# Causal mask of the first attention pass moved into constant rows of its contraction, with a reordered word list

## The reference

```python
att = jnp.einsum('bhqd,bhkd->bhqk', q, k) * (1.0 / math.sqrt(HS))
causal = jnp.tril(jnp.ones((Tx, Tx), bool))
att = jnp.where(causal[None, None, :, :], att, jnp.float32(-10000000000.0))
att = jax.nn.softmax(att, axis=-1)
y = jnp.einsum('bhqk,bhkd->bhqd', att, v)
y = y.transpose(0, 2, 1, 3).reshape(Bx, Tx, Cx)
return y @ Wp + bp
...
x = x + _layernorm(_L0_attn_ref(_layernorm(x, axis=-1), ...), axis=-1)
x = x + _layernorm(_L0_ffn_ref(_layernorm(x, axis=-1), ...), axis=-1)
```

## Time and profile before

| | |
|---|---|
| Median of 3 runs | 1155.79 us (1154.74 to 1156.82) |
| Span of the profiled execution | 1155.0 us |
| Own time of the profiled execution | not given apart from its span |
| TensorE busy | 1089.6 us, 94% |
| GpSimd busy | 833.4 us, 72% |
| VectorE busy | 832.6 us, 72% |
| ScalarE busy | 736.3 us, 64% |
| Mean granted TensorE clock | 0.967 |

### The profile page before, as it was taken

The page is one execution under the profiler, slowest core; times in us unless marked ns, Lnnn a source line. Parts: engine busy times, 40 slices in busy tenths (PEclk is TensorE's granted clock), DMA queues, the critical chain, the costliest instruction groups (busy, mean ns, idle before and its releaser), DMA issues.

```text
span 1155.0 us, 26958 instructions
## 1 busy us (share of the span) xinstructions
PE 1089.6 (94%) x8484; PEld 693.7 (60%) x8484; DVE 832.6 (72%) x2263; ACT 736.3 (64%) x1617; POOL 833.4 (72%) x972
## 2 busy tenths in 40 slices
...
GB/s 96 119 156 46 136 90 63 114 73 136 109 70 114 58 122 93 119 110 60 117 59 137 97 86 105 60 132 35 120 157 84 100 174 134 133 173 136 109 243 197
DMA packets 108885, 129.13 MB, mean 112 GB/s; under 512 B 17627, under 2 KB 89548, under 8 KB 104140
## 3 DMA queue, kind: packets, MB, share of 16 engines
...
q10 hardware_dynamic: 390, 0.10, 0.0%
...
## 4 chain that ended last, share of the span: by engine, by line
PE 89%; DVE 3%; DMA 2%; POOL 2%; SPq 2%; issue 1%; ACT 1%; POOLq 0%; DVEq 0%; ACTq 0%
PE heads_ps L1508 14%; PE score L1498 13%; PE wide L1536 12%; PE wide L1648 8%; PE wide L1474 6%; PE wide L1538 5%; PE score L1486 4%; PE wide L1631 3%; PE wide L1632 3%; PE score L1622 3%; PE misc L1516 3%; PE wide L1569 2%; DVE mx L1299 1%; PE wide L1576 1%; PE wide L1589 1%
## 5 line engine op out<-in xcount | busy, mean ns | idle before, releaser
L961 ACT ACTIVATE values<-score 128x512 f32<-128x512 f32 (+1 forms) x704 | 371.3, 558 | 122.7 <-PE score L1498 112.4
L1299 DVE TENSOR_REDUCE mx<-wide 128x2 f32<-128x1024 f32 (+3 forms) x384 | 392.9, 1042 | 73.4 <-PE wide L1538 69.0
L1536 PE MATMUL wide<-qk 72*128 72x512 bf16 (+3 forms) x1024 | 246.5, 305 | 8.0 <-DVE mx L1299 4.5
L871 POOL TENSOR_SCALAR_AFFINE_SELECT values<-values 128x512 f32<-128x512 f32 x256 | 173.9, 688 | 109.8 <-ACT values L961 108.4
L1498 PE MATMUL score<-qk 75*128 75x512 bf16 (+3 forms) x1024 | 230.1, 301 | 1.5 <-ACT values L961 0.8
L1538 PE MATMUL wide<-maskneg,identb 128*128 128x128 bf16 x1024 | 198.4, 222 | 0.0
L916 POOL DMA_INDIRECT token_scratch<-spread,e_id x144 | 137.7, 956 | 72.8 <-issue 52.9
L1508 PE MATMUL heads_ps<-values 128*32 128x512 f32 (+3 forms) x2048 | 175.4, 444 | 0.0
L860 POOL DMA_INDIRECT sorted_scratch<-zr,places x128 | 133.5, 1043 | 37.3 <-issue 28.5
L1536 PEld LDWEIGHTS wide<-qk 72*128 72x128 bf16 x1024 | 100.9, 99 | 79.4 <-issue 17.4
L1498 PEld LDWEIGHTS score<-qk 75*128 75x128 bf16 x1024 | 87.3, 98 | 97.6 <-ACT values L961 46.8
...
## 6 DMA issues: line engine op xcount, KB each, us to landing
...
```

The costliest lines, as they stand in the source:

```text
L871: nc.gpsimd.affine_select(out=prob[n][:, :, 0:P], in_=prob[n][:, :, 0:P], compare_op=ALU.is_ge, fill=0.0, base=0, pattern=[[0, HG], [1, P] ...
L961: nc.scalar.activation(free_ap(prob[kb][:, hs_[0], :], [[1, N * len(hs_)]]), score[SCORE_RING.buffer(b, step)][:, 0:N * len(hs_)], ACT.Exp ...
L1299: nc.vector.tensor_reduce(mx[:, h0:h0 + len(hs_), j:j + 1], src, axis=AX.X, op=ALU.max).then_inc(p1_max, 1)
L1536: nc.tensor.matmul(o, q4[e][0:ROWS, h, j * P:(j + 1) * P], k4[e][0:ROWS, h, 0:L], start=True, stop=False)
```

## The change

Outside the lists, the mask leaves the second matmul and becomes part of the contraction. 43 further rows (75 to 117, up to `MROWS` = 118) of `q4` and `k4` hold constant staircases, each row stepping at three positions, whose products are huge and negative above the diagonal. A pair of the first pass is now, for j over 0, a matmul with 72 rows over the j*128 columns that need no mask, and for every j one with 118 rows over the 128 columns of the diagonal block. `identb` and `maskneg` go. Since the 118 rows take in rows 72 to 74, those must be zero in `q4` until the maxima are laid in, so `shuffle` gets a seventh transfer for each half, which writes zeros. The staircases are made on GpSimd by six selects, four of them behind a wait, and copied once over all heads into partitions 64 to 127 of the four tiles: two copies of 8192 columns on VectorE (`stairs0`, `stairs2`) and two on ScalarE (`stairs1`, `stairs3`), as words of `START`. The two transfers of ones move from ScalarE to SyncE, in front of the first shuffles and behind waits for the copies. `ORDER` holds the same 160 words in a new order.

```diff
--- before.py
+++ after.py
@@ -20,13 +20,16 @@
 NPART = 3
 ROWS = NPART * NPART * HS
 SROWS = ROWS + NPART
+STAIR = 3
+MROWS = SROWS + -(-P // STAIR)
+HALF_ROWS = 64
+AHEAD, APART = 2.0 ** 34, 2.0 ** 46
 TOPK = 2
 ROW = P + 5
 EVEN = 112
 CAP = 72 * P
 BG = 4
 ROUND = 4
-NEG = -1e30
 EPS = 1e-5
 FILL = 12
 FIRST_FILL = 12
@@ -90,18 +93,17 @@
 
 
 ORDER = (
-    "s0.0 v3.1@-1 mask2.1 s0.1 p18@0 s0.2 p19@0 s0.3 v3.2@-1 v3.3@-1 p20@0 s0.4 s0.5 rnormal heads3@-1 p21@0 "
-    "mask2.2 s0.6 s0.7 p22@0 s0.8 K p23@0 s0.9 place s0.10 cos Y v0.0 M1@0 s1.0 s1.1 N1@0 p0 W mask2.3 s1.2 rstd "
-    "s1.3 v0.1 H2 v0.2 v0.3 zstats O1@0 s1.4 p1 normal mask3.0 U1 G1 s1.5 p2 s1.6 v1.0 p3 d3 s1.7 mask3.1 s1.8 p4 "
-    "mask3.2 d4 s1.9 p5 mask3.3 d5 s1.10 heads0 third0 s2.0 third1 p6 s2.1 p7 s2.2 v1.1 s2.3 p8 s2.4 v1.2 v1.3 "
-    "sin0@4 p9 d6 d7 s2.5 s2.6 U2 H0@-1 sin1@4 mask0.0@1 rstats mask0.1@1 G2 p10 sin2@4 heads1 s2.7 mask0.2@1 "
-    "mask0.3@1 stats d0@-1 s2.8 V s2.9 s2.10 p11 d1@-1 T v2.0 s3.0 mask1.0@1 p12 s3.1 d2@-1 M0 zrstd@0 v2.1 s3.2 "
-    "N0 p13 sin3@4 O0 Z@0 s3.3 rX v2.2 v2.3 mask1.1@1 residual@0 s3.4 p14 choose s3.5 second rL heads2 s3.6 p15 "
-    "s3.7 chosen rexp X@4 v3.0 s3.8 mask1.2@1 mask1.3@1 R@4 s3.9 U0@-1 G0@-1 p16 s3.10 mask2.0@1 D H1@-1 rrstd@0 "
-    "Q@4 p17 "
+    "s0.0 v3.1@-1 mask2.1 rnormal s0.1 p18@0 s0.2 p19@0 s0.3 v3.2@-1 v3.3@-1 mask2.2 s0.4 p20@0 s0.5 mask2.3 "
+    "heads3@-1 s0.6 p21@0 s0.7 p22@0 s0.8 K s0.9 rstd p23@0 H2 place v0.0 s0.10 Y s1.0 cos p0 s1.1 normal M1@0 W d3 "
+    "s1.2 s1.3 v0.1 N1@0 zstats v0.2 v0.3 s1.4 O1@0 p1 s1.5 G1 mask3.0 U1 third0 p2 mask3.1 s1.6 v1.0 p3 s1.7 s1.8 p4 "
+    "d4 s1.9 p5 s1.10 heads0 s2.0 p6 d5 s2.1 d6 p7 s2.2 d7 v1.1 mask3.2 s2.3 s2.4 p8 mask3.3 v1.2 H0@-1 sin0@4 v1.3 "
+    "sin1@4 p9 mask0.0@1 sin2@4 s2.5 third1 s2.6 rstats sin3@4 G2 mask0.1@1 U2 p10 heads1 s2.7 d0@-1 s2.8 V d1@-1 "
+    "s2.9 stats s2.10 p11 T v2.0 mask0.2@1 s3.0 p12 s3.1 mask0.3@1 d2@-1 mask1.0@1 M0 v2.1 N0 zrstd@0 p13 s3.2 s3.3 "
+    "Z@0 rX v2.2 O0 mask1.1@1 v2.3 p14 s3.4 residual@0 s3.5 rL choose mask1.2@1 s3.6 p15 s3.7 rexp mask1.3@1 H1@-1 "
+    "mask2.0@1 R@4 chosen G0@-1 rrstd@0 heads2 second X@4 s3.8 U0@-1 D p16 s3.9 v3.0 s3.10 Q@4 p17 "
 )
 START = (
-    "rstd@1 X@1 stats@1 Q@1 normal@1 cos@1 sin0@1 stats@2 V sin1@1 T@1 sin2@1 splits@1 second@1 sin3@1 X@2 fold@1 "
+    "stairs1@1 rstd@1 X@1 stats@1 stairs0@1 Q@1 normal@1 cos@1 stairs2@1 sin0@1 stats@2 V stairs3@1 sin1@1 T@1 sin2@1 splits@1 second@1 sin3@1 X@2 fold@1 "
     "R@1 rstd@2 normal@2 Q@2 cos@2 X third0@1 third1@1 stats@3 sin0@2 rstd@3 p0 p1 p2 normal@3 sin1@2 p3 T@2 "
     "second@2 sin2@2 sin3@2 Q p4 R@2 third0@2 sin0 p5 p6 p7 third1@2 p8 cos p9 sin1 sin2 sin3 R p10 rstd stats "
     "normal third0 p11 third1 sin0@4 p12 p13 mask0.0@1 mask0.1@1 M0 sin1@4 mask0.2@1 p14 mask0.3@1 mask1.0@1 "
@@ -225,8 +227,8 @@
             return free_ap(flat, [[a, b] for a, b in zip(steps, dims)], offset)
 
         ident = sb("ident", [P, P])
-        identb = sb("identb", [P, P], BF16)
-        maskneg = sb("maskneg", [P, P], BF16)
+        stairs = sb("stairs", [P, 2, P], BF16)
+        zero_row = sb("zero_row", [NPART, T], BF16)
         share = sb("share", [P, P], BF16)
         bp_rows = sb("bp_rows", [P, P], BF16)
         bp_part = sb("bp_part", [P, P], BF16)
@@ -261,8 +263,8 @@
         parts = view(spread, BF16, [2, NPART, T], 2 * 2 * T)
 
         qk4 = sb("qk4", [P, 4, NH, T], BF16)
-        q4 = [qk4[0:96, 2 * n, :, :] for n in range(2)]
-        k4 = [qk4[0:96, 2 * n + 1, :, :] for n in range(2)]
+        q4 = [qk4[0:MROWS, 2 * n, :, :] for n in range(2)]
+        k4 = [qk4[0:MROWS, 2 * n + 1, :, :] for n in range(2)]
         VEXT = NT * NH * 32
         values = sb("values", [P, 2 * VEXT + HG * (NT * T - P * NT * (NT - 1) // 2)])
         vext = [view(values, F32, [NT, NH, 32], n * VEXT) for n in range(2)]
...
@@ -340,7 +344,8 @@
         x1_ready = sem("x1_ready")
         x1_out = sem("x1_out")
 
-        N_SHUFFLE = 2 * NPART * 16
+        N_SHUFFLE = (2 * NPART + 1) * 16
+        N_STAIR = 6
         N_W = 10 * 16
         x_v = x.rearrange("b (t p) c -> b p t c", p=P)
         flat = lambda ap: ap.rearrange("p t c -> p (t c)")
...
@@ -630,6 +635,7 @@
                     sp.dma_start(k4[e][rows, hs_, :],
                                  bass.AP(k_all.tensor, k_all.offset + at, [[NH * T, HS], [P * T, NPART], [1, NH // 2 * T]])
                                  ).then_inc(shuffled[e][half], 16)
+                sp.dma_start(q4[e][ROWS:SROWS, hs_, :], free_ap(zero_row[:], [[0, NH // 2], [1, T]])).then_inc(shuffled[e][half], 16)
 
             def body(i):
                 e = i % 2
@@ -672,7 +678,10 @@
                     wait(sp, p2_scores, i * P2_N * NG + P2_N * NG // 2)
                     apart(sp)
                     if i < 0:
-                        sp.wait_ge(rows_filled, 32)
+                        sp.wait_ge(k_stairs, i + 3)
+                        sp.wait_ge(q_stairs, i + 3)
+                        wait(sp, rows_filled, 16 * (i + 2))
+                        sp.dma_start(k4[e][ROWS:SROWS, :, :], free_ap(onesb[0:NPART, :], [[0, NH * NT], [1, P]])).then_inc(rows_filled, 16)
                     sp.wait_ge(parts_out, 16 * (i + 3))
                     shuffle(i + 2, e, 0)
                 if exists(i, -1):
@@ -767,7 +776,7 @@
 
         @block.gpsimd
         def _(pool):
-            for m, s in ((ident, 0.0), (identb, 0.0), (maskneg, 0.0), (before, 1.0), (upto, 1.0), (onesb, 1.0)):
+            for m, s in ((ident, 0.0), (stairs, 0.0), (before, 1.0), (upto, 1.0), (onesb, 1.0), (zero_row, 0.0)):
                 nc.gpsimd.memset(m[:], s).then_inc(ident0, 1)
             nc.gpsimd.memset(mhalf[:], -0.5).then_inc(ident0, 1)
             nc.gpsimd.memset(share[:], 1.0 / 32).then_inc(ident0, 1)
@@ -780,11 +789,6 @@
                            allow_small_or_imprecise_dtypes=True).then_inc(ident_ready, 1)
             nc.gpsimd.affine_select(out=ident[:], in_=ident[:], compare_op=ALU.not_equal, fill=1.0, base=0,
                                     pattern=[[-1, P]], channel_multiplier=1).then_inc(ident_ready, 1)
-            nc.gpsimd.affine_select(out=identb[:], in_=identb[:], compare_op=ALU.not_equal, fill=1.0, base=0,
-                                    pattern=[[-1, P]], channel_multiplier=1).then_inc(ident_ready, 1)
-
-            nc.gpsimd.affine_select(out=maskneg[:], in_=maskneg[:], compare_op=ALU.is_ge, fill=NEG, base=0,
-                                    pattern=[[-1, P]], channel_multiplier=1).then_inc(ident_ready, 1)
             nc.gpsimd.iota(iota_e[:], pattern=[[1, E]], base=0, channel_multiplier=0,
                            allow_small_or_imprecise_dtypes=True).then_inc(ident_ready, 1)
             nc.gpsimd.iota(iota_blk[:], pattern=[[1, NBLK]], base=0, channel_multiplier=0,
@@ -794,6 +798,20 @@
                                     pattern=[[1, P]], channel_multiplier=-1).then_inc(ident_ready, 1)
             nc.gpsimd.affine_select(out=upto[:], in_=upto[:], compare_op=ALU.is_ge, fill=0.0, base=0,
                                     pattern=[[1, E]], channel_multiplier=-1).then_inc(ident_ready, 1)
+
+            def stair(side, compare, ahead, value, steps):
+
+                if steps:
+                    pool.wait_ge(ident_ready, N_IDENT + steps)
+                nc.gpsimd.affine_select(out=stairs[:, side, :], in_=stairs[:, side, :], compare_op=compare, fill=value,
+                                        base=STAIR * SROWS - ahead, pattern=[[1, P]], channel_multiplier=-STAIR).then_inc(ident_ready, 1)
+
+            stair(1, ALU.not_equal, 0, 1.0 / APART, 0)
+            stair(0, ALU.is_ge, 0, -AHEAD * APART, 0)
+            stair(1, ALU.not_equal, 1, 1.0, 1)
+            stair(0, ALU.not_equal, 0, -AHEAD, 2)
+            stair(1, ALU.not_equal, 2, APART, 3)
+            stair(0, ALU.not_equal, 1, -AHEAD / APART, 4)
 
             def inverse_deviation(out_, var, added, before, done, sums=vareps):
 
@@ -940,9 +958,7 @@
         @block.scalar
         def _(act):
 
-            act.wait_ge(ident_ready, N_IDENT)
-            for n in range(2):
-                act.dma_start(k4[n][ROWS:SROWS, :, :], free_ap(onesb[0:NPART, :], [[0, NH * NT], [1, P]])).then_inc(rows_filled, 16)
+            act.wait_ge(ident_ready, N_IDENT + N_STAIR)
             def body(i):
                 for step in steps_at(i, B):
                     if not exists(i, step.offset):
@@ -1024,6 +1040,9 @@
                         act.wait_ge(qk_transposed, b + 1)
                         wait(act, parts_out, 16 * b)
                         nc.scalar.activation(parts[:, :, 0, :], unit[:], ACT.Copy).then_inc(part1_ready, 1)
+                    elif step.what == "stairs" and n % 2 == 1:
+                        nc.scalar.activation(free_ap(qk4[HALF_ROWS:P, n - 1, 0, :], [[P, NH * NT], [1, P]]),
```

(16 more changed lines are left out.)

4 lines of the change are left out of this document (3 added, 1 removed).

## The result

The changed kernel takes **1135.09 us** (median of 4 runs, 1133.13 to 1136.48) where the kernel before takes 1155.74 (1154.74 to 1156.82), a ratio of 0.9818 (95% interval 0.9805 to 0.9831). It is faster by 20.6 us. I had forecast 1110, faster by 45.7, with a range from 1101 to 1132: the sign held, the time lies 3 us above the range, and less than half of the forecast gain came.

The account below looks back on a forecast made before the run. TensorE, streaming without gaps, was taken to bound the iterations. From 1155.8 us, 53.4 came off for removed columns, 4.5 came back for stalls and 3.5 for the start, giving 1110 us, range 1101 to 1132.

Parts of the forecast that it names:

- Columns removed: First-pass matmul pairs on TensorE: 3.5 us less per iteration, 53.4 us in all; START's 18 units worth nothing.
- Rivals 3 and 4: First-pass matmuls: 3, weight loads come into the open, 1140 us, chance 0.03; 4, row changes drain TensorE, 1236, 0.04.
- What is late next: Iterations: period 46.3 us, GpSimd at 93% with waits shrinking, tight `wide` buffers; 4.5 us back in all.
- The small places: Iterations: three places short by 0.1 us each on TensorE, 0.3 in each of 15 iterations, 4.5 us back.
- the ring of `wide`: The pair of `wide` buffers: p5 may start only when p3's maximum is out; short by 0.1 us.
- The start: Ahead of p0: ScalarE copy 1.3 us late, VectorE copies 1.5 exposed, seventh transfer's issue 0.6; about 3.5 us lost.
- Rival 2: Iterations: GpSimd and VectorE take over in part, stalls of 1.0 to 2.0 us each; 1131 us (1118 to 1140), chance 0.19.
- Rival 1: Whole kernel: everything hidden, no stall in iterations and 1 us at the start; 1103 us (below 1105), chance 0.14.
- The sum: Whole kernel: 1155.8 - 53.4 + 4.5 + 3.5 = 1110 us; 1105 to 1118 given chance 0.60.
- The signs named: Profile after: matmul counts, W 46.3 to 46.8 us apart, TensorE busy throughout, GpSimd's mask waits near 2, p0 at 49.
- The clock's sign: START, a sign of being wrong: clock at its lower level beyond 75 us, costing up to 7 us more.

Follow-up runs that it names:

- the best kernel: The changed kernel with mask0.2@1 and mask0.3@1 in front of d0@-1 and START's staircase copies moved out of GpSimd's way: 1112.22 us, ratio 0.9635.
- last experiment: The best kernel with word p8 moved in front of s2.4 instead of behind it: 1112.43 us, ratio 0.9632.
- the second chip: The changed kernel, unaltered, run again on another chip: 1135.59 us beside 1155.2, ratio 0.9831.

## Why the prediction was right and wrong

**Columns removed: right.** 3.5 us per iteration were forecast. The first pass takes 3.07 less from start to start, but its 9.56 us hold 0.24 of waits, 0.18 of them in front of T for ScalarE's eviction of V, and 0.18 of entries to tiles of v, which stand behind p words at two places now and behind other words before (11 entries of 0.09 in both lists). Without them the columns gave 3.49. The wait in front of T, in the best kernel:

```profile
324.13 0.42 PEld L1607 LDWEIGHTS wide<-ident,front 128*128 128x128 f32 x4 [0.19 <-ACT values L1034]
```

Matmuls of 118 rows stand at the pace of their columns beside those of 72. Rivals 3 and 4 fall with that row: a drain of 0.09 us for each change of rows would have made 8.6 us per iteration, and the first pass would have grown.

**What is late next: the step that failed.** I counted GpSimd's work (41.4 us), saw that it fits into 46.3, and wrote that its waits for exponentials vanish when TensorE comes sooner, and that "the order of TensorE's words is otherwise nearly the old one". The first came true by half (3.8 us of such waits in an iteration before, 1.9 after), the second is true, and neither asks the question that mattered: which words stand in front of a mask on GpSimd now, and for what they wait. The diff shows mask0.2@1 and mask0.3@1 behind `d0@-1` and `d1@-1`; the earlier trace rows shows that in an iteration `d` was held by nothing but its issue in the old place, so its dependence on VectorE's `places` has no row there. The list over the whole span of the kernel before does have it, from two waits at 848 and 871 us:

```profile
L860 POOL DMA_INDIRECT sorted_scratch<-zr,places x128 | 133.5, 1043 | 37.3 <-issue 28.5 <-DVE places L1231 7.9 <-PE score L1486 0.6
```

Beside the order of the words that row would have given the question. The price was 1.17 us per iteration, 16.5 us in all, against the 0.3 per iteration that I had put down for all stalls. Moving the two masks back, on a chip without late signals, shows this by itself.

**The small places: about right in kind, a third of their size.** With the masks in front the period is 47.24 instead of the 46.6 that the forecast had (46.3 + 0.3). The columns account for 49.78 - 3.5 = 46.28, so small waits take 0.96: 0.30 in front of U2, 0.18 in front of T, 0.11 in front of `heads`, most others 0.05 to 0.10. In the changed kernel they and the 1.17 of the masks make 2.1, past even the 2 that I had taken for the range. I had looked at the ring of `wide` and found 0.1 short; the largest place was the same ring at another word, and its maximum waited for VectorE's stream, not for the p word (last experiment).

**The start: mis-sized, and in other terms than I had.** Forecast 3.5, measured 5.6 at the first p0 and 4.4 at the first word of the iterations, s0.0 (81.92 instead of 77.55); from p0 to s0.0, where START's own 18 units lie, pass 30.5 us instead of 31.7, and I had those units at nothing. ScalarE's copies took 7.03 us each as worked out (7.0) and cost nothing: the first began at 5.34 rather than 7.35, and in front of both following evictions ScalarE idled (2.62 and 3.41 us) for TensorE. The seventh transfer is the last to land in front of p0, but from the issue of the sixth to p0 pass 7.0 us in the changed kernel and 7.1 in the best one where it was 6.8, so it costs 0.2 at most and not its 0.64. VectorE's two copies, which I had a quarter exposed (1.5), were exposed for 2.0 each, and 1.6 more came from Q at half clock, which I had nowhere. The Trainium skill (VectorE: DVE Perf Modes, "The perf-mode tier table") gave an estimated 2.2 us for a copy, and 2.29 was measured; its page SBUF — State Buffer ("Who interferes with whom") says that such a copy and a GpSimd instruction exclude each other, and `vareps` at 2.22 instead of 0.23 agrees. My 3 us for a copy was high, my quarter of it exposed low.

**The rivals.** Rival 2 (1118 to 1140, GpSimd and VectorE take over in part) has the time, and its sign was there: weight loads waiting for masks, W 48 us apart. Its mechanism was only half right: it spoke of GpSimd's waits coming from its position in the list, and so it was, but the wait was for VectorE's `places` and not for exponentials, and the load was no part of it. With the masks in front, GpSimd is busier (41.03 of 47.20) and nothing stalls on it. Rival 1, everything hidden at 1103, was reached by no kernel.

**The sum, remade.** Of the 25.6 us between the forecast and the changed kernel's 1135.6 on the second chip 16.5 are the two masks, and 6.8 are the start with its copies out of GpSimd's way (two chips, whose times for the kernel before differ by 1.0). The 2 us left between 1110 and 1112.2 are two larger differences that nearly cancel: the period of 47.24 instead of 46.6 costs about 15 x 0.6 = 9, and s0.0 comes at 75.37, 2.2 earlier than before where I had it 3.5 later, which gives back 5.7. So the best kernel's agreement with the forecast is in part luck. The remaining 1 to 2 us are within the spread of the executions (1110.57 to 1113.61).

**The signs named.** 768 matmuls of 72 rows and 1024 of 118, the latter followed after 0.06: seen. GpSimd's waits in front of masks near 2 us per iteration: seen, 9.3 us in five iterations, and they told nothing, since the wait that cost time stood in front of `d0`. TensorE busy all through, W 46.3 to 46.8 apart, p0 at 49: not seen, but 47.42 of 48.40, 48.42 and 51.4. The clock's sign was there in the changed kernel, at a granted clock of 0.50 from 75.3 to 80.6 us where it had been 1.00, but s0.0 came 4.4 later too; the best kernel has 1.00 from 73.2 on.
